# A four-layer cross-attention kernel on one core: another order around the third layer's MLP

## The chip, the cores and the metric

One core of a Trainium2 chip runs the whole kernel. The metric is the device time of one launch in microseconds. Everything is float32 at the interface; TensorE (PE) multiplies, VectorE (DVE), ScalarE (ACT) and GpSimd (POOL) do the rest, and SyncE (SP) issues the transfers.

## What is computed

Eight sequences `b` of 256 tokens, width 256, pass through four cross-attention layers that all look at the same context of 8 x 64 tokens. The third layer (called layer 2 here, counted from 0) is the one that matters:

```python
x = layer_norm(hidden_states, ln1_w, ln1_b)
q, k, v = x @ q_w + q_b, ctx @ k_w + k_b, ctx @ v_w + v_b      # 16 heads of 16
attn = softmax(where(mask, q @ k.T * scale, lowest))
hidden = (attn @ v) @ cproj_w + cproj_b + hidden_states
y = layer_norm(hidden, ln2_w, ln2_b)
y = gelu(y @ fc_w + fc_b, approximate=True) @ proj_w + proj_b  # the MLP, 256 -> 1024 -> 256
x = hidden + y
```

Layer 0 and layer 1 are attention alone; the fourth layer has two cross-attentions with 16 heads of 128 and an MLP of its own.

## The kernel before, in words

**Slots.** Layers 0 to 2 are cut into 24 units, one for each layer and sequence, so units 16 to 23 are layer 2. Every engine runs the same loop over slots `u = 0..25`, each with its own list of steps written out by hand, and semaphores alone tie the engines together. An engine works its list strictly in order. A unit of layer 2 has two tiles of 128 x 1024 scores. In slot `u` TensorE does: scores of unit `u`, `source(u+2)` (transposes of the normalised input into `work[2]`, L436), `values(u+1)` (L481), `probs_transposed` (L561), `reciprocals_transposed(u-1)` into `work[3]` (L575), `weighted(u-1)` (L594), `queries(u+1)` (L518) and last `output(u-1)` (L610). VectorE does in slot `u`: `mlp_weight_low(u-18)` (L1161), `unit_residual(u-2)` (L1118), in slots 21 to 23 `mlp_stats` (L1004, L1008), `tile_sums` of the last tile (L1092), `unit_reciprocals` (L1099), `tile_max` and `tile_shifted` for two tiles (L1070, L1086) with `mlp_norm` (L1014) between them in slots 21 to 23, `unit_normal(u-1)` (L1105) and `tile_sums` of the first tile. `source(u+2)` in layer 2 waits for `unit_residual(u-2)`, which frees `work[2]`, and for the normalised input of `ln_finish` on ScalarE (L1568). GpSimd halves and quarters the exponentials for the sums (L1898, L1901), spreads the reciprocals (L1888), finishes the variances (`rstd`, L1857 and L1860) and adds bias rows (L1910).

**The MLP in parts.** A float32 product is made of three in a rounded format: high x high, low x high and high x low (L631 to L633). ScalarE rounds (`mlp_weight_high` L1611, `mlp_source_high` L1623, `mlp_hidden` L1722 with the gelu and L1728 with the rounding) and VectorE subtracts to get the low part (`mlp_weight_low`, `mlp_source_low` L1175, `mlp_hidden_low` L1180). The weights are eight pieces; ScalarE rounds piece `u-17` at the end of slot `u`, and VectorE's low part of it stands at the start of slot `u+1`.

**Order around the MLP.** For a sequence `b` there are four `hidden(b, f)` (12 matmuls of 256 columns each, into `fbank[f]`, the two halves of the two score tensors) and one `projected(b)` (48 matmuls, into `work[b % 2]`). In slot 24, with no scores left, TensorE does `mlp_source(0)` (into `fbank[3]`), the last probabilities, `reciprocals_transposed(23)`, `weighted(23)`, `hidden(0,0)` and `output(23)`, then `hidden(0,1..3)` with `mlp_source(1)` before the last. From then on a pass is `hidden(b,0)`, `hidden(b,1)`, `mlp_source(b+1)`, `projected(b-1)`, `hidden(b,2)`, `hidden(b,3)`. `mlp_hidden(0,·)` on ScalarE waits until `output(23)` is done, since its buffers lie over attention buffers.

VectorE's pass `b` is: `mlp_hidden_low(b,0)`, `mlp_affine(b+1)` (L1020), `mlp_hidden_low(b,1)`, `mlp_source_low(b+1)`, then work for the fourth layer's weights, which it does in passes 2 to 6: `wq_biased` in 3 to 6 (L1293, 128 x 1024), `wq_sums` in 2 to 5 (L1285, four) and `value_sums` in 2 to 5 (L1307, four, each on the result of the one before). Then `mlp_residual(b-1)` (L1270), `mlp_hidden_low(b,2)` and `(b,3)`, and `mlp_stats(b+3)` with `mlp_norm(b+3)`, between which VectorE waits for GpSimd's `rstd`. GpSimd has `mlp_bias` (L1910) behind each norm and `wq_scaled` (L1986) behind each `wq_sums`.

**After it.** The fourth layer's loop over `STEPS` starts with `key_projection(0)`, which waits until all MLP residuals are done (`d_mr`), and `key_projection(1)` (L775), then `key_products(0)`, `key_products(1)` (L847). On ScalarE `key_bias(1)` (L1758) stands behind the copies of `key_products(0)` (L1768). SyncE loads the fourth layer's value weights when `projected(7)` is done, since they lie over the MLP's weights.

## Time and profile before

| what | value |
| --- | --- |
| median of 3 runs | 1130.79 us (1129.34 to 1131.52) |
| the profiled execution: its own time / its span | 1130.49 / 1128.4 us |
| PE busy | 1033.0 us, 92% |
| DVE busy | 663.2 us, 59% |
| ACT busy | 519.1 us, 46% |
| POOL busy | 402.6 us, 36% |

The rows further down are of this profiled execution, times in us from the start of its span; 2.1 us of its time lie outside the span. The share of the whole hides the stage: slots 18 to 24 of the loop run from about 303 to 391 us, the MLP from there to about 501 us. In a timeline row the bracket holds how long the engine was idle before the operation and what released it. PEclk is the granted TensorE clock as a share of 2.4 GHz.

### The profile page before, as it was taken

Reading aid. Unit: us, or ns where it says so; the run is one execution under the profiler, and the core shown is the slowest. Engines: PE = TensorE matmul, PEld = TensorE weight load, DVE = VectorE, ACT = ScalarE, POOL = GpSimd, SP = SyncE. Lnnn points to the kernel's source line nnn. Section 1 sums busy time; section 2 is a strip of 40 time slices with the busy share of each in tenths; the row PEclk is TensorE's granted clock in tenths of the full one; section 3 lists DMA queues with packets and bytes.
Section 4 is the critical chain, followed back from the end, with each engine's and each line's share of the span. In section 5 each row is a group of like instructions: output and inputs, shape, how many; then the busy total and the mean of one; then the engine's idle time right before and its main releaser. Section 6 shows DMA issues by size and latency. Waiting matters only on the chain.

```text
span 1128.4 us, 17672 instructions
## 1 busy us (share of the span) xinstructions
PE 1033.0 (92%) x7036; PEld 810.7 (72%) x7036; DVE 663.2 (59%) x1127; ACT 519.1 (46%) x1036; POOL 402.6 (36%) x416
## 2 busy tenths in 40 slices
PE   6999889887789799989999999999999999978997
PEld 3666555555566699887787777777777777648997
DVE  3657888778568669722444545775444454574552
ACT  2556777676566454433333332333323333324543
POOL 2534578688966523200222112331122211222230
PEclk9999999998999999999999999999999999999999
DMA  9000000000000060010000013310000000100000
GB/s 307 36 2 1 1 1 1 1 1 1 1 1 1 24 220 1 1 53 23 1 1 1 1 49 102 112 38 1 1 1 1 1 1 7 69 1 1 29 19 29
DMA packets 17046, 32.26 MB, mean 29 GB/s; under 512 B 3522, under 2 KB 8388, under 8 KB 16452
## 3 DMA queue, kind: packets, MB, share of 16 engines
q1 hardware_dynamic: 16964, 31.13, 8.1%
q8 instruction: 56, 0.92, 0.3%
q14 instruction: 26, 0.21, 0.1%
HBM read 29.03 MB, written 2.10 MB: 28 GB/s over the span
## 4 chain that ended last, share of the span: by engine, by line
PE 74%; ACT 8%; POOL 7%; issue 5%; DVE 5%; DMA 0%; POOLq 0%; DVEq 0%; ACTq 0%
PE work L775 10%; PE work L891 10%; PE scores L830 9%; PE work L847 5%; PE work L880 4%; PE work L561 3%; PE work L631 3%; PE work L632 3%; PE work L633 3%; PE scores L631 3%; PE scores L633 3%; PE scores L632 2%; PE work L518 2%; PE work L862 2%; PE work L436 2%
## 5 line engine op out<-in xcount | busy, mean ns | idle before, releaser
L891 PE MATMUL work<-pair,probsT 128*128 128x256 f32 x512 | 120.3, 388 | 11.0 <-ACT pair L1777 8.8
L1857 POOL TENSOR_SCALAR stat<-stat 128x2 f32<-128x2 f32 (+1 forms) x49 | 11.1, 227 | 315.4 <-DVE stat L1008 313.9
L891 PEld LDWEIGHTS work<-pair,probsT 128*128 128x128 f32 x512 | 95.7, 192 | 35.3 <-issue 20.3
L775 PE MATMUL work<-ctxT,w 128*128 128x128 f32 x1008 | 118.2, 275 | 2.7 <-ACT pair L1777 1.1
L775 PEld LDWEIGHTS work<-ctxT,w 128*128 128x128 f32 x1008 | 116.3, 192 | 4.1 <-issue 2.0
L830 PE MATMUL scores<-pair,act_bufs 128*128 128x512 f32 x256 | 115.2, 592 | 0.0
L1768 ACT ACTIVATE pair<-work 128x512 f32<-128x512 f32 x64 | 38.2, 598 | 154.5 <-PE work L847 154.5
L1758 ACT ACTIVATE kvT<-work,cols 128x128 f32<-128x128 f32 x124 | 35.5, 369 | 153.2 <-PE work L775 153.2
L2005 POOL TENSOR_TENSOR probs<-probs,smax 128x1024 f32<-128x1024 f32 x22 | 42.0, 1907 | 157.6 <-DVE smax L1398 157.6
L1378 DVE TENSOR_REDUCE smax<-scores 128x16 f32<-128x1024 f32 x32 | 39.2, 1225 | 77.2 <-PE scores L830 77.2
L830 PEld LDWEIGHTS scores<-pair,act_bufs 128*128 128x128 f32 x256 | 46.3, 190 | 46.0 <-issue 45.9
L1369 DVE TENSOR_TENSOR kvT<-work,cols 128x512 f32<-128x512 f32 x32 | 22.1, 691 | 93.1 <-PE work L775 93.1
L847 PEld LDWEIGHTS work<-kvT,w 128*128 128x128 f32 x512 | 61.9, 192 | 15.4 <-issue 15.4
L1070 DVE TENSOR_REDUCE smax<-scores 128x16 f32<-128x1024 f32 x48 | 57.9, 1205 | 20.1 <-PE scores L552 19.4
L847 PE MATMUL work<-kvT,w 128*128 128x128 f32 x512 | 62.4, 275 | 1.8 <-ACT kvT L1758 1.8
L880 PE MATMUL work<-w,kvT 128*64 128x256 f32 x512 | 62.3, 385 | 0.0
L561 PEld LDWEIGHTS work<-ident,pair 128*128 128x128 f32 x256 | 30.0, 150 | 40.6 <-ACT pair L1579 30.6
L561 PE MATMUL work<-ident,pair 128*128 128x128 f32 x256 | 37.7, 294 | 22.1 <-ACT w L1586 13.3
L1586 ACT ACTIVATE w<-work 128x512 f32<-128x512 f32 x88 | 47.6, 593 | 14.4 <-PE work L561 14.3
L1910 POOL TENSOR_TENSOR x<-x,rows_late 128x512 f32<-128x512 f32 x32 | 50.2, 1572 | 9.9 <-DVE act_bufs L1014 8.2
L1014 DVE TENSOR_SCALAR act_bufs<-x,stat 128x256 f32<-128x256 f32 x58 | 44.0, 800 | 14.9 <-POOL stat L1860 14.9
L1898 POOL TENSOR_TENSOR pair<-probs 128x512 f32<-128x512 f32 x32 | 40.9, 1278 | 29.8 <-ACT probs L1579 29.6
(194 smaller groups left out, 2634.0 us busy)
## 6 DMA issues: line engine op xcount, KB each, us to landing
w<-in_l_wk SPq DMA_DIRECT2D x8, 512.0 KB, 6.1
w<-in_l_wq SPq DMA_DIRECT2D x8, 512.0 KB, 6.7
w<-in_l_wo SPq DMA_DIRECT2D x8, 512.0 KB, 7.5
w<-in_l_wv SPq DMA_DIRECT2D x8, 512.0 KB, 5.4
out<-x SPq DMA_DIRECT2D x8, 256.0 KB, 2.2
x<-in_x SPq DMA_DIRECT2D x1, 1536.0 KB, 9.3
pair<-in_l_fc SPq DMA_DIRECT2D x1, 1024.0 KB, 7.1
pair<-in_l_pr SPq DMA_DIRECT2D x1, 1024.0 KB, 9.1
```

Source lines behind the costliest of these rows:

```text
L561: last = tr(work[half][:, q * P:(q + 1) * P], probs[k % 4][:, (4 * half + q) * P:(4 * half + q + 1) * P], ident[:, :])
L631: mm(bank, s_hi, m_hi, start=start, stop=False)
L632: mm(bank, s_hi, m_lo, start=False, stop=False)
L633: return mm(bank, s_lo, m_hi, start=False, stop=stop)
L775: last = mm(bank[:, h * P:(h + 1) * P], w[:, c, (4 * g + h) * K3:(4 * g + h + 1) * K3], ctxT[:, c, p * P:(p + 1) * P], start=(c == 0), sto ...
L830: last = mm(sc[j % 2][:, half * BANK:(half + 1) * BANK], fixed[j // 2 % 2][:, c, t * P:(t + 1) * P], pk[n % 2][:, bb, c, half * BANK:(half ...
L847: last = mm(step_banks(j)[2 + c][:, h * P:(h + 1) * P], w3_wq[:, 4 * g + h, c * P:(c + 1) * P], kvT[i % 2][:, h, :], start=True, stop=True)
L880: last = mm(bank[h * S:(h + 1) * S, bb * D:(bb + 1) * D], kvT[2][:, 2 * q + h, bb * S:(bb + 1) * S], w3_wo[:, 4 * g + 2 * q + h, :], start ...
L891: last = mm(step_banks(j + 1)[0][:, 0:D], probsT_bufs[j % 2][:, q, :], pv[n % 2][:, bb, q, :], start=(q == 0), stop=(q == GH // 2 - 1))
L1070: v.tensor_reduce(smax[k % 2][:, 0:GH], s3, X, ALU.max).then_inc(d_max, 1)
L1586: act(pT[:, 4 * half:4 * half + 4, t, :], work[half][:, :].rearrange("p (q n) -> p q n", n=P), ACT.Copy).then_inc(a_pT, 1)
L1910: g.tensor_tensor(xb(b), xb(b), row(name).unsqueeze(1).broadcast_to([P, TT, D]), ALU.add).then_inc(done, 1)
```

## The change

1. Slots 18 to 25: `mlp_weight_low` moves from the start of VectorE's slot to its end.
2. `mlp_source(0)` moves from slot 24 to slot 23, ahead of `output(22)`, and from `fbank[3]` to `work[3]`; `reciprocals_transposed(23)` now waits for its affine step. VectorE's `mlp_affine(0)` stands first in slot 24 and `mlp_source_low(0)` ahead of the last tile's sums; ScalarE's `mlp_source_high(0)` ahead of the last `probs_out`.
3. `hidden(0,0)` goes ahead of `reciprocals_transposed(23)`, `hidden(0,1)` in between `weighted(23)` and `output(23)`; both wait for the second last tile alone.
4. Statistics and norm of sequence 2 leave slot 23: a pass `b` of the MLP now does `mlp_stats(b+2)`, `mlp_norm(b+2)`, and in another place.
5. A pass on TensorE is `hidden(b,0)`, `hidden(b,1)`, `mlp_source(b+1)`, `hidden(b,2)`, `projected(b-1)`, `hidden(b,3)`. VectorE takes `mlp_hidden_low(b,2)` ahead of statistics, norm and the weight work, and `mlp_residual(b-1)`, `mlp_hidden_low(b,3)` last. GpSimd takes `wq_scaled` behind `mlp_bias`.
6. `key_projection(0)` and `(1)` go ahead of `projected(7)`, into `fbank[0]` and `fbank[1]`, and wait for the gelus of those banks; the wait for all residuals moves to the steps behind.

```diff
         def key_bank(i):
-            return fbank[0] if i == 1 else step_banks(i - 4)[0]
+            return fbank[i] if i < 2 else step_banks(i - 4)[0]
...
+        def mlp_bank(b):
+            return work[3] if b == 0 else work[2 + b % 2]
...
+                if u == NU - 1:
+                    e.wait_ge(d_mT, 2)
...
-                    e.wait_ge(d_seen, NK)
+                    e.wait_ge(a_rT, NU - 1)
...
-                    e.wait_ge(d_seen, NK)
+                    e.wait_ge(d_seen, NK - 1 + f // 2)
...
-                    if u == NU:
-                        mlp_source(0)
                     for k in late:
                         probs_transposed(k)
                     if tiles:
                         scores(*tiles_of(u)[1])
+                    if u == NU:
+                        hidden(0, 0)
                     if u > 0:
                         reciprocals_transposed(u - 1)
                         weighted(u - 1)
                     if u == NU:
-                        hidden(0, 0)
+                        hidden(0, 1)
...
+                if u == NU - 1:
+                    mlp_source(0)
                 if u > 0:
                     output(u - 1)
...
-            for f in range(1, 4):
-                hidden(0, f)
-                if f == 2:
-                    mlp_source(1)
-            for b in range(1, B + 1):
-                for f in range(2):
-                    if b < B:
-                        hidden(b, f)
+            hidden(0, 2)
+            mlp_source(1)
+            hidden(0, 3)
+            for b in range(1, B):
+                hidden(b, 0)
+                hidden(b, 1)
                 if b + 1 < B:
                     mlp_source(b + 1)
+                hidden(b, 2)
                 projected(b - 1)
-                for f in range(2, 4):
-                    if b < B:
-                        hidden(b, f)
+                hidden(b, 3)
...
-                if i == 0:
-                    e.wait_ge(d_mr, B)
-                if i == 1:
-                    e.wait_ge(a_g, 4 * B)
+                if i < 2:
+                    e.wait_ge(a_g, 4 * (B - 1) + i + 1)
...
+            for i in range(2):
+                key_projection(i - 4, i)
+            projected(B - 1)
...
-                for q in mlp_pieces(u - 1):
-                    mlp_weight_low(q)
+                if u == NU:
+                    mlp_affine(0)
                 if u >= 2:
                     unit_residual(u - 2)
-                if NU - 3 <= u < NU:
+                if u == NU:
+                    mlp_source_low(0)
+                if NU - 3 <= u < NU - 1:
                     mlp_stats(u - NU + 3)
-                if u == NU:
-                    mlp_affine(0)
...
-                if NU - 3 <= u < NU:
+                if NU - 3 <= u < NU - 1:
                     mlp_norm(u - NU + 3)
...
-                if u == NU:
-                    mlp_source_low(0)
                 if tiles:
                     tile_sums(tiles[0][0])
+
+                for q in mlp_pieces(u - 1):
+                    mlp_weight_low(q)
...
-            for b in range(B + 1):
-                if b < B:
-                    mlp_hidden_low(b, 0)
+            for b in range(B):
+                mlp_hidden_low(b, 0)
                 if b + 1 < B:
                     mlp_affine(b + 1)
-                if b < B:
-                    mlp_hidden_low(b, 1)
+                mlp_hidden_low(b, 1)
                 if b + 1 < B:
                     mlp_source_low(b + 1)
+                mlp_hidden_low(b, 2)
+                if b + 2 < B:
+                    mlp_stats(b + 2)
+                    mlp_norm(b + 2)
...
                 if b > 0:
                     mlp_residual(b - 1)
-                for f in range(2, 4):
-                    if b < B:
-                        mlp_hidden_low(b, f)
-                if b + 3 < B:
-                    mlp_stats(b + 3)
-                    mlp_norm(b + 3)
+                mlp_hidden_low(b, 3)
+            mlp_residual(B - 1)
...
+                    if u == NU:
+                        mlp_source_high(0)
                     for k in late:
                         probs_out(k)
...
-            for b in range(3):
+            for b in range(2):
                 mlp_bias(b)
-            for b in range(3, B):
-                if b >= 5:
-                    wq_scaled(1, b - 5)
+            for b in range(2, B):
                 rstd(("m2", b), TT)
                 mlp_bias(b)
-            wq_scaled(1, 3)
+                if b >= 4:
+                    wq_scaled(1, b - 4)
```

## Rows read from the trace of the kernel before

**Rows 1.** What TensorE waited for, 290 to 520 us: total, times, longest.

```profile
PE work L436 <- DVE x L1118: 7.8, 4, 3.5
PE work L631 <- ACT m_hid_high L1728: 6.5, 3, 2.4
```

**Rows 2.** Timeline, slot 18: start, duration, engine, operation, [idle before, releaser].

```profile
305.12 1.09 ACT L1568 ACTIVATE act_bufs<-x,stat 128x256 f32<-128x256 f32 x2 [2.38 <-POOL stat L1866]
...
306.76 0.89 DVE L1161 TENSOR_TENSOR m_w_low<-pair,m_w_high 128x512 fp32r<-128x512 f32 x1 [5.17 <-ACT m_w_high L1611]
...
308.31 0.66 PE L436 MATMUL work<-ident,act_bufs 128*128 128x128 f32 x4 [3.53 <-DVE x L1118]
...
308.89 1.98 PE L481 MATMUL work<-w,ctxT 128*64 128x256 f32 x8
```

**Rows 3.** Timeline, slot 20, 334 to 335 us.

```profile
334.25 0.68 DVE L1118 TENSOR_TENSOR x<-work,x 128x512 f32<-128x512 f32 x1
...
334.98 0.66 PE L436 MATMUL work<-ident,act_bufs 128*128 128x128 f32 x4 [1.42 <-DVE x L1118]
```

**Rows 4.** Timeline, slots 23 and 24, 373 to 387 us.

```profile
373.43 1.13 DVE L1014 TENSOR_SCALAR act_bufs<-x,stat 128x256 f32<-128x256 f32 x2
...
377.60 3.42 PE L610 MATMUL work<-w,pair 128*128 128x256 f32 x8 [1.85 <-DVE pair L1105]
...
379.53 1.06 POOL L1901 TENSOR_TENSOR pair<-pair 128x256 f32<-128x256 f32 x1
...
381.06 0.69 DVE L1118 TENSOR_TENSOR x<-work,x 128x512 f32<-128x512 f32 x1 [1.05 <-PE work L610]
...
384.09 0.66 PE L575 MATMUL work<-ident,pair 128*128 128x128 f32 x4 [1.76 <-POOL pair L1888]
...
386.42 0.68 DVE L1175 TENSOR_TENSOR m_src_low<-act_bufs,m_src_high 128x512 fp32r<-128x512 f32 x1
```

**Rows 5.** Timeline behind `output(23)`, 390 to 398 us.

```profile
390.70 1.28 ACT L1722 ACT_TABLE_LOAD   x1 [4.80 <-PE work L610]
...
392.86 0.63 ACT L1728 ACTIVATE m_hid_high<-pair 128x512 fp32r<-128x512 f32 x1
...
393.40 0.82 ACT L1722 ACTIVATE pair<-scores,cols 128x256 f32<-128x256 f32 x2
...
397.62 0.55 PE L631 MATMUL scores<-m_src_high,m_w_high 128*128 128x256 f32 x1 [2.29 <-ACT m_src_high L1623]
```

**Rows 6.** Windows: stretch, length, busy us of PE, PEld, DVE, ACT, POOL, then PEclk.

```profile
397.62:401.00 3.38, 3.38 (x16) 3.38 (x17) 2.12 (x7) 1.01 (x3) 0.95 (x2) 0.50 1.01 384
402.06:414.00 11.94, 11.94 (x103) 11.94 (x102) 6.90 (x12) 6.12 (x14) 1.00 (x1) 1.00 0.82 321
439.44:453.64 14.20, 12.81 (x95) 12.84 (x96) 12.95 (x28) 4.85 (x11) 5.17 (x4) 0.88 0.01 2
```

**Rows 7.** Timeline of VectorE and GpSimd in the MLP's `b = 4`.

```profile
442.75 0.74 DVE L1014 TENSOR_SCALAR pair<-x,stat 128x256 f32<-128x256 f32 x2 [1.14 <-POOL stat L1860]
...
446.30 1.22 DVE L1293 TENSOR_TENSOR w<-w,pair 128x1024 f32<-128x1024 f32 x1
...
449.06 4.06 DVE L1307 SCALAR_TENSOR_TENSOR pair<-w,cols,pair 128x256 f32<-128x256 f32 x4
...
443.56 1.66 POOL L1910 TENSOR_TENSOR x<-x,rows_late 128x512 f32<-128x512 f32 x1 [0.85 <-DVE pair L1014]
449.23 2.58 POOL L1986 TENSOR_TENSOR w<-w,pair 128x1024 f32<-128x1024 f32 x1 [4.00 <-DVE pair L1285]
```

**Rows 8.** One line's view: `value_sums` at L1307, duration min/median/max in ns.

```profile
L1307 DVE SCALAR_TENSOR_TENSOR pair<-w,cols,pair x30: 466/485/2506, 421.2 to 771.4; 128x256 f32<-128x256 f32 x30
```

**Rows 9.** Timeline at the end of the MLP, 501 to 511 us.

```profile
501.68 2.02 PE L775 MATMUL work<-ctxT,w 128*128 128x128 f32 x16 [0.87 <-DVE x L1270]
...
509.08 2.02 PE L847 MATMUL work<-kvT,w 128*128 128x128 f32 x16 [1.81 <-ACT kvT L1758]
```

**Rows 10.** DMA issues on the page: KB each, median us to landing.

```profile
w<-in_l_wv SPq DMA_DIRECT2D x8, 512.0 KB, 5.4
```

More of the change, by code:

```diff
@@ L645, in mlp_source @@
                     e.wait_ge(d_mT, 2 * (b - 2) + 2)
-                transposes(fbank[3] if b == 0 else work[2 + b % 2], norm[(B + b) % 3]).then_inc(pe_mx, 1)
+                transposes(mlp_bank(b), norm[(B + b) % 3]).then_inc(pe_mx, 1)
             def hidden(b, f):
@@ L779, in first_free @@
             def first_free(j):
+                e.wait_ge(d_mr, B)
                 e.wait_ge(a_pk, 2 * keys_before(j))
@@ L785, in second_free @@
             def second_free(j):
+                e.wait_ge(d_mr, B)
                 e.wait_ge(a_pk, 2 * keys_before(j))
@@ L790, in third_free @@
             def third_free(j):
+                if j > -4:
+                    e.wait_ge(d_mr, B)
                 e.wait_ge(a_lk, keys_before(j))
@@ L794, in fourth_free @@
             def fourth_free(j):
+                if j > -4:
+                    e.wait_ge(d_mr, B)
                 e.wait_ge(d_vT, values_before(j))
@@ L907, in value_constants @@
                 mm(step_banks(j)[1][:, 0:D], ones[:, :], value_sum, start=True, stop=True).then_inc(pe_bias, 1)
+            for i in range(2):
+                key_projection(i - 4, i)
+            projected(B - 1)
             for j in STEPS:
                 key, value, i = key_of(j), value_of(j), input_of(j)
-                if key is not None and key != 1:
+                if key is not None and key >= 2:
                     key_projection(j, key)
-                if key == 0:
-                    key_projection(j + 1, 1)
                 if value is not None:
@@ L1169, in mlp_affine @@
                     e.wait_ge(a_sh, b - 2)
-                affine(fbank[3] if b == 0 else work[2 + b % 2], srcT[i % 3], "l2_g2", "l2_b2", d_mT)
+                affine(mlp_bank(b), srcT[i % 3], "l2_g2", "l2_b2", d_mT)
             def mlp_source_low(b):
@@ L1688, in scalar @@
                         exponentials(tiles[0])
-                if u == NU:
-                    mlp_source_high(0)
                 if u > 0:
@@ L1730, in scalar @@
             for b in range(B):
-                mlp_hidden(b, 0)
-                mlp_hidden(b, 1)
-                if 0 < b and b + 1 < B:
-                    mlp_source_high(b + 1)
-                mlp_hidden(b, 2)
-                if b == 0:
-                    mlp_source_high(1)
+                for f in range(3):
+                    mlp_hidden(b, f)
+                    if f == (2 if b == 0 else 1) and b + 1 < B:
+                        mlp_source_high(b + 1)
                 mlp_hidden(b, 3)
@@ L1970, in gpsimd @@
                     reciprocals_spread(u - 1)
-                if NU - 3 <= u < NU:
+                if NU - 3 <= u < NU - 1:
                     rstd(("m2", u - NU + 3), TT)
```

## The prediction

> **What bounds the kernel now.** I read the waits of TensorE first, since the table has it busy for 92% of the span: from 290 to 520 us two entries stand out, `source` waiting for `unit_residual` (L436, 7.8 us in four waits) and `projected` waiting for the low hidden parts (L631, 6.5 us in three) [rows 1]. Then the timeline at each of them. In slot 18 the transposes start at 308.31 after 3.53 us of idle TensorE. The engine named is VectorE, but its residual is itself queued behind `mlp_weight_low` (L1161), which had stood idle 5.17 us for ScalarE's rounded piece [rows 2]. In slot 20 the same order costs 1.42 us [rows 3], and so it does in 19 and 21 (7.8 - 3.53 = 4.27 = 3 x 1.42) [rows 1, 3]. In slots 23 and 24 VectorE's own list is the chain. In the MLP one pass takes 14.20 us, of which VectorE is busy 12.95 and waits 1.14 for GpSimd's `rstd`; that is the whole of it, while TensorE needs 11.94 us for a pass [rows 6, 7]. So passes 3 to 5 go by VectorE, although the waits name ScalarE.
>
> **Part 1, low weight parts at the slots' ends.** Slot 18: the residual can start when `output(16)` is done, about 303.7. Next late is the normalised input of `source(20)`, which ScalarE finishes at 305.12 + 1.09 = 306.2 [rows 2]. The transposes go at 306.3 instead of 308.31: 2.0 us. Behind the long wait TensorE ran at half clock: `values` took 1.98 us [rows 2], eight matmuls that run in about 1.1 at full clock; the matmuls behind them in the same 3.4 us lose another 0.5. With a wait of 1.5 us left, like the 1.42 in slot 20, I take this away too: 1.4 us, bounds 0 and 1.4, the upper because the row it is nearest to, slot 20, shows no such loss. Slots 19 to 21: the residual starts with the end of `output`, 1.2 us ahead of the end of the scores that TensorE does meanwhile, so the transposes follow without a gap: 4.3 us. TensorE is then the bound there, at 12.55 - 1.42 = 11.1 us a slot; VectorE has 8.6 to 9.7 of work. The moved subtraction itself (0.89 in [rows 2]) falls into VectorE's idle time at the slot's end; its input is by then a slot old. In slots 21 and 22 VectorE leads or starts 0.3 us sooner: 0.5 together. Sum of part 1: 2.0 + 1.4 + 4.3 + 0.5 = 8.2.
>
> **Part 2, slots 23 and 24.** VectorE's list in slot 23 loses `mlp_stats(2)` (0.9) and `mlp_norm(2)` (1.1, L1014) [rows 4]. `output(22)` waits for `unit_normal(22)` at the end of this list (1.85 us, behind another short wait, and then 3.42 us at half clock for eight matmuls that take 1.9) [rows 4]. It starts 1.85 us sooner, at 375.75 on the old time scale, now with `mlp_source(0)` in the gap before it, and ends at 377.7, not 381.0. From there on VectorE: sums, the low part, `mlp_affine(0)` (1.0) to 377.7, `unit_residual(22)` to 378.4, `mlp_source_low(0)` (0.68) [rows 4] to 379.1, sums of the last tile (GpSimd done by 378.7; before, 379.53 + 1.06 = 380.6 [rows 4]), reciprocal at 379.8, GpSimd's spread 380.45. TensorE: last probabilities, `hidden(0,0)` from 379.15 to 380.6, `reciprocals_transposed(23)` at 380.6 (was 384.09 [rows 4]), weighted to 382.25, `hidden(0,1)` to 383.7, `output(23)` to 385.6. Before, `hidden(0,0)` stood behind `mlp_source_low(0)` at 386.42 [rows 4] and `output(23)` ended at 390.6. Gain 5.0. `hidden(0,1)` delays `output(23)` by 0.7, which is in the sum. The new wait of `reciprocals_transposed(23)` for the affine step has `weighted`, `hidden(0,1)` and `output(23)` behind it; the step is done 2.8 us earlier, so it costs nothing, and at most the step's 1.0 if that lead were gone. On ScalarE the last `probs_out` stands behind `mlp_source_high(0)`, which waits for that same step until 377.7; the transposes that it copies come at 378, so nothing is lost.
>
> **Part 3, up to `hidden(1,0)`.** Nothing is gained. `hidden(1,0)` needs source 1, and ScalarE starts on that only after a table load of 1.28, three gelus (0.82) with three roundings (0.63), all behind `output(23)` [rows 5]: 397.62 - 390.6 = 7.0 us, before and after. TensorE only waits longer for it, 3.6 us for 2.29, and then runs at half clock as now (16 matmuls in 3.38 us, PEclk 0.50 [rows 6], a loss of 1.5).
>
> **Part 4, the MLP's passes.** Three `hidden` ahead of `projected` give TensorE 1.43 us more cover. But the bound is VectorE's pass, and its list doesn't get shorter. It is 14.20 [rows 6], plus two things. First, `mlp_hidden_low(b,2)` now stands directly behind `mlp_source_low`, where before the weight work stood: ScalarE needs 0.63 for the source, 0.82 and 0.63 for the gelu [rows 5], VectorE has 1.3 us of work meanwhile, so it waits 0.8. Second, GpSimd's `mlp_bias` (L1910) starts just behind the norm [rows 7]; before, short steps lay beside it, now `wq_biased` and `wq_sums` do. What such a meeting costs VectorE the trace shows for `value_sums`: 0.485 us each, but up to 2.506 [rows 8], and four take 4.06 while GpSimd's 2.58 us run begins [rows 7], so VectorE stands still for GpSimd's whole instruction. For `wq_sums` (L1285) there is no such meeting in the trace. Bounds: 0, or the 1.25 us that L1910 runs; a little below 0 (-0.2) if the short steps now go free of it. I take 1.25, since L1307 reads two float32 operands from SBUF just as L1285 does. Pass: 14.20 + 0.8 + 1.25 = 16.25. Statistics now lie in passes 2 to 5 beside the weight work, so three such periods follow on pass 2. Counted from `hidden(1,0)`: VectorE starts pass 2 at 16.5 and needs 14.5 (as above without `wq_biased`) up to `mlp_hidden_low(2,3)`; `projected(2)`, which TensorE reaches at 30.1, starts at 31.8, `projected(5)` at 31.8 + 3 x 16.25 = 80.5. Behind it TensorE is the bound: 5.84 + 1.5 (half clock after a wait of 4) + 4 x 1.43 + 5.84 + 1.43 + 3.7 (two key projections) + 5.84 = 29.9, to 110.4. Before, the same work ended at 501.68 + 2 x 1.9 [rows 9] = 505.5, or 107.9. So the passes lose 2.5, after they got back 5 us at the end, where the wait ahead of `projected(7)`, its half clock and the 0.87 us for the residual [rows 9] go.
>
> The Trainium skill has a rule for this meeting (page SBUF — State Buffer, section "Who interferes with whom"): a VectorE instruction with two inputs in SBUF contends with a GpSimd instruction that reads SBUF, and the one that issued first blocks the other for its whole length. L1307 agrees. By the rule `wq_sums` would be blocked as well, the 16.25; without it the pass would be 15.0.
>
> **Part 5, the key projections.** `key_products(0)` can follow `projected(7)` at once, but `key_bias(1)` stands behind its copies on ScalarE's list as before, so the 1.81 us wait of L847 [rows 9] stays. The residual of sequence 7 (0.7) hides behind `key_products(0)` (1.8). The value weights' transfers are issued with the end of `projected(7)`, as before; they land 5.4 us after issue [rows 10], and `value_projection(0)` now comes 8.2 us behind it instead of 12.9: nothing, or up to 1 us if the first lands late. All behind that shifts as a whole.
>
> **Sum.** 8.2 + 5.0 + 0 - 2.5 + 0 = 10.7 us. The profiled execution took 1130.49 (span 1128.4, the rest outside), 0.3 below the median. 1130.5 - 10.7 = 1119.8 us.
>
> **Rivals.**
> A. `wq_sums` isn't held up by GpSimd. For it: none of its instructions shows it; against: L1307 [rows 8]. Four passes are 1.25 shorter: 1114.8.
> B. The slots don't close. What is late next there (ScalarE's `ln_finish`, the exponentials, GpSimd, idle only 0.5 us between some steps in slot 18) takes the place of the residual, and slot 18 keeps its half clock: 4.3 + 1.4 less, 1125.5.
> C. The cover does all that it could and TensorE sets the passes: `projected(5)` at 30.1 + 3 x 11.94 = 65.9, the end at 94.3: 13.6 gained where I lose 2.5, 1103.7. Against it stands VectorE's 12.95 us of work in a pass [rows 6], over 11.94.
> D. Slower. TensorE now stands 4.3 us ahead of each `projected` in four passes and 3.6 ahead of `hidden(1,0)`. If the clock stays at the lower of its two levels (1.2 GHz) for the whole pass, a pass takes 2 x 11.94 = 23.9, over 16.25: 7.6 each, 30 us in four, 1150. It makes the kernel slower from 15 us at the lower level in each pass on (half of it lost, less the 4.3 idle, four times, over 10.7 + 2.3). Against it: after waits of 2.3 to 3.5 us the clock was back within 3.4 us [rows 2, 6].
> E. Gains and losses cancel (B with a longer list on VectorE than counted): 1130.
>
> **How the numbers follow.** About 0.2% can be told from no change here. Forecast 0.50 (own range 1117 to 1122.5), A 0.22 (1112 to 1117), B 0.15 (1123 to 1127.5), C 0.03, D 0.05, E 0.05. Leaving out C, D, E and the outer part of B gives 1112.5 to 1126. Faster by over 0.2%: 0.50 + 0.22 + 0.15 + 0.03 = 0.90; same 0.05; slower 0.05.
>
> **What would show it.** Right: no wait of L436 on L1118 above 0.3 us in slots 19 to 21, 306.3 for the transposes in slot 18, `output(23)` ending 13 us sooner, `projected(2)` to `projected(5)` 16.2 us apart with waits of 3 to 4 us ahead of them, L1285 with durations above 1.5 us, no wait ahead of `projected(7)`, the 1.8 us wait of L847 still there. Wrong: passes of 15.0 (A), of 12 (C), or long matmuls through a whole pass (D).

## The result and the profile after

The changed kernel takes **1119.29 us** (median of 4 runs, 1118.81 to 1119.43) where the kernel before took 1131.15 beside it (4 runs, 1129.34 to 1131.60): ratio 0.9897, 95% interval 0.9880 to 0.9914. It is 1.0% faster, 0.5 us from the forecast of 1119.8. Its profiled execution took 1119.15 us, with a span of 1117.0 (before: 1130.49 and 1128.4).

The span falls into four parts, cut at three starts that every kernel here has: `output(16)`, `output(23)` and the first key product. The last columns are the lengths between the cuts. All experiments are in it too, since most verdicts below are read here. Each row is one profiled execution; in e2 and e9 it is the fastest of four, 4.2 and 3.1 us or more under the other three.

| kernel | output(16) starts | to output(23) | to the first key product | to the end | span |
|---|---|---|---|---|---|
| before | 301.70 | 87.00 | 116.62 | 623.08 | 1128.4 |
| **changed** | 303.31 | 74.03 | 116.67 | 622.99 | 1117.0 |
| e1_low_first | 303.93 | 81.79 | 119.23 | 626.05 | 1131.0 |
| e2_low_last_alone | 302.15 | 77.61 | 112.25 | 623.19 | 1115.2 |
| e3_narrow_bias | 301.96 | 74.01 | 115.34 | 623.39 | 1114.7 |
| e4_old_passes | 302.84 | 75.23 | 112.55 | 625.78 | 1116.4 |
| e5_keys_behind | 302.86 | 74.02 | 121.81 | 627.81 | 1126.5 |
| e6_spread | 302.64 | 74.02 | 103.63 | 625.11 | 1105.4 |
| e7_spread_early | 302.32 | 74.02 | 102.13 | 623.23 | 1101.7 |
| e8_old_slot24 | 302.57 | 75.18 | 115.70 | 625.85 | 1119.3 |
| e11_delay_1 | 302.12 | 74.02 | 120.23 | 625.13 | 1121.5 |
| e9_delay_2 | 302.72 | 74.06 | 118.43 | 624.69 | 1119.9 |
| e10_delay_4 | 302.14 | 74.05 | 120.04 | 625.87 | 1122.1 |

Of the 11.4 us, 12.97 were gained in slots 18 to 24 (87.00 to 74.03), nothing in the MLP (116.62 and 116.67), and nothing in the fourth layer (623.08 and 622.99). The first column lost 1.6: the changed execution was already 1.37 us later at its first `output` (41.83 for 40.46). The three delay kernels, whose code is the changed kernel's up to there, have that row at 40.77 to 41.25, so the first stage differs by about a microsecond between executions of the same order of work.

The waits of TensorE from 290 to 515 us, changed kernel (total, times, longest), answer to [rows 1]:

```profile
PE work L637 <- issue: 10.0, 4, 3.9
PE work L440 <- ACT act_bufs L1576: 4.1, 2, 2.5
PE scores L637 <- ACT m_src_high L1631: 3.7, 1, 3.7
PE work L856 <- issue: 1.8, 1, 1.8
```

The residual is gone from the list: `source` (now L440) waits for the normalised input alone. The waits ahead of `projected` (L637 to `work`) grew to 10.0 us and are put down to "issue". What ends them is VectorE's low hidden part: in the pass shown below the two at 433.09 take 1.28 us together, the first is done at about 433.8, and `projected(3)` starts at 433.87.

Slot 18, timeline (start, duration, engine, operation, idle before and releaser), answers to [rows 2]:

```profile
305.24 0.69 DVE L1128 TENSOR_TENSOR x<-work,x 128x512 f32<-128x512 f32 x1 [2.04 <-PE work L616]
...
306.71 1.09 ACT L1576 ACTIVATE act_bufs<-x,stat 128x256 f32<-128x256 f32 x2 [2.37 <-POOL stat L1871]
...
307.95 0.63 PE L440 MATMUL work<-ident,act_bufs 128*128 128x128 f32 x4 [1.57 <-ACT act_bufs L1576]
...
308.51 1.08 PE L485 MATMUL work<-w,ctxT 128*64 128x256 f32 x8
```

The residual starts as soon as `output` ends, the wait fell from 3.53 to 1.57, and `values` runs in 1.08 us at full clock (1.98 before). Behind `output(23)`, answering to [rows 5] and [rows 6] (in the second fence: stretch, length, busy us of PE, PEld, DVE, ACT, POOL, then PEclk, the granted clock):

```profile
379.34 1.28 ACT L1730 ACT_TABLE_LOAD   x1 [3.30 <-PE work L616]
...
386.26 0.51 PE L637 MATMUL scores<-m_src_high,m_w_high 128*128 128x256 f32 x1 [3.72 <-ACT m_src_high L1631]
```

```profile
433.87:449.90 16.03, 13.65 (x101) 13.48 (x101) 13.98 (x28) 6.26 (x13) 5.72 (x4) 0.89 0.01 2
```

A pass takes 16.03 us now. VectorE is busy 13.98 of it, and most of the rest are two waits (0.70 and 1.14 us) that its timeline shows. The rows are from the pass ahead of that window, `b = 3`, VectorE and then GpSimd, answering to [rows 7]:

```profile
421.37 0.69 DVE L1190 TENSOR_TENSOR m_hid_low<-pair,m_hid_high 128x512 fp32r<-128x512 f32 x1 [0.70 <-ACT m_hid_high L1736]
...
424.09 0.74 DVE L1024 TENSOR_SCALAR act_bufs<-x,stat 128x256 f32<-128x256 f32 x2 [1.14 <-POOL stat L1865]
424.74 1.22 DVE L1303 TENSOR_TENSOR w<-w,pair 128x1024 f32<-128x1024 f32 x1
425.87 1.53 DVE L1295 CUSTOM_DVE_ANT_0 pair<-w,pair,cols 128x256 f32<-128x256 f32 x1
...
427.33 0.47 DVE L1295 CUSTOM_DVE_ANT_0 pair<-w,pair,cols 128x256 f32<-128x256 f32 x1
...
428.55 4.02 DVE L1317 SCALAR_TENSOR_TENSOR pair<-w,cols,pair 128x256 f32<-128x256 f32 x4
...
433.09 1.28 DVE L1190 TENSOR_TENSOR m_hid_low<-pair,m_hid_high 128x512 fp32r<-128x512 f32 x2
...
424.91 2.21 POOL L1915 TENSOR_TENSOR x<-x,rows_late 128x512 f32<-128x512 f32 x1 [0.85 <-DVE act_bufs L1024]
428.71 2.54 POOL L1991 TENSOR_TENSOR w<-w,pair 128x1024 f32<-128x1024 f32 x1 [1.59 <-DVE pair L1295]
```

And the end of the MLP, TensorE, answering to [rows 9]: no wait for the residual is left, that of the key products is.

```profile
494.01 1.95 PE L856 MATMUL work<-kvT,w 128*128 128x128 f32 x16
497.72 2.02 PE L856 MATMUL work<-kvT,w 128*128 128x128 f32 x16 [1.76 <-issue]
```

### The profile page after: what moved, and what is told of

Same layout as the page of the kernel before. It is cut to its first block, busy times and chain, and to the rows that moved or that the text cites. A ratio compares the mean times of both kernels' runs of the same rounds, so it can differ in the third digit from the quotient of the medians.

```text
span 1117.0 us, 17673 instructions
## 1 busy us (share of the span) xinstructions
PE 1030.6 (92%) x7036; PEld 809.2 (72%) x7036; DVE 663.2 (59%) x1127; ACT 518.3 (46%) x1036; POOL 403.5 (36%) x416
## 4 chain that ended last, share of the span: by engine, by line
PE 76%; ACT 7%; POOL 7%; issue 5%; DVE 4%; DMA 0%; POOLq 0%; DVEq 0%; ACTq 0%
PE work L900 10%; PE work L780 10%; PE scores L839 10%; PE work L856 5%; PE work L889 4%; PE work L565 3%; PE work L637 3%; PE work L638 3%; PE work L639 3%; PE scores L637 3%; PE work L522 3%; PE scores L639 3%; PE scores L638 3%; PE work L616 2%; PE work L440 2%
## 5 line engine op out<-in xcount | busy, mean ns | idle before, releaser
L565 PE MATMUL work<-ident,pair 128*128 128x128 f32 x256 | 36.5, 288 | 20.1 <-ACT w L1594 11.9
L1594 ACT ACTIVATE w<-work 128x512 f32<-128x512 f32 x88 | 47.4, 592 | 10.7 <-PE work L565 10.7
```

The costliest lines, as they stand in the source:

```text
L565: last = tr(work[half][:, q * P:(q + 1) * P], probs[k % 4][:, (4 * half + q) * P:(4 * half + q + 1) * P], ident[:, :])
L1594: act(pT[:, 4 * half:4 * half + 4, t, :], work[half][:, :].rearrange("p (q n) -> p q n", n=P), ACT.Copy).then_inc(a_pT, 1)
```

## Experiments: what each part is worth

The expectations number the parts as the six items of the section on the change; the prediction's part 4 is items 4 and 5, its part 5 is item 6.

**Item 1 taken back.** The low weight parts stand ahead of the residual again, all else as changed.

```
                     tile_shifted(*tiles[0])
+                for q in mlp_pieces(u - 1):
+                    mlp_weight_low(q)
                 if u == NU:
                     mlp_affine(0)
...
-                for q in mlp_pieces(u - 1):
-                    mlp_weight_low(q)
```

> The changed kernel (1119.3 us) with the low weight parts back at the start of VectorE's slots 18 to 25, all else as changed. My account: what queues the residual behind ScalarE's rounded piece is this position alone, worth 2.0 + 1.4 in slot 18, 1.42 each in slots 19 to 21 and 0.5 in 21 and 22, so 8.2 us are lost: 1127.5 us, and source(20) to source(23) again wait on the residual (about 3.5, 1.4, 1.4, 1.4). Rival: most of the slots' gain comes from elsewhere or is given back at the MLP's passes, which VectorE sets: 1120 to 1122 us.

Measured: 1133.02 us (6 runs, 1130.14 to 1136.21), ratio to before 1.0018 (0.9998 to 1.0037). The whole gain is gone, which is more than item 1. The table says which share is its own: the slots take 81.79 for 74.03, 7.8 us (expected 8.2), and the waits for the residual are back:

```profile
PE work L440 <- DVE x L1128: 7.2, 4, 3.0
```

The other 5.6 us (2.56 up to the first key product, 3.06 behind it) lie where no order was changed. `projected(5)` to `projected(6)` took 13.06 us for 11.56 and `output(23)` to `projected(0)` 16.31 for 15.24, for the same matmuls: TensorE's clock, taken up below.

**Item 1 alone**, in the kernel before: the same two lines moved to the slot's end, nothing else.

> The kernel before (1131.2 us) with this one edit alone, the low weight parts at the end of the slots. My account: 8.2 us, 1123.0 us, output(20) about 8 us earlier, and the rest of the kernel shifted as a whole with MLP passes of 14.2 us as before. Rival: the gain needs the new order of slots 23 and 24 behind it, 1127 us or more.

Measured: 1121.52 us (4 runs, 1117.27 to 1121.66), ratio 0.9907 (0.9889 to 0.9926). The slots went from 87.00 to 77.61: item 1 alone is worth 9.4 us of the 12.97, and 7.8 when it comes last, since in slots 23 and 24 it and item 4 relieve the same list. The passes stayed at 14.2 us. The MLP was 4.4 shorter than in the kernel before though its order is the same; three stretches of half clock of some 1.45 us each did not come in this execution. It took 1117.27 us at a mean granted clock of 0.986, the other three executions of the same kernel 1121.48 to 1121.66 at 0.982. By the medians item 1 alone gives 10.0 us (1131.49 beside it) and all six items 11.9.

**Items 2 and 3 taken back**: source 0 and the first two slices of the hidden layer at their old places, on all engines.

```
+                    if u == NU:
+                        mlp_source(0)
                     for k in late:
                         probs_transposed(k)
...
-                    if u == NU:
-                        hidden(0, 0)
                     if u > 0:
                         reciprocals_transposed(u - 1)
                         weighted(u - 1)
                     if u == NU:
-                        hidden(0, 1)
+                        hidden(0, 0)
...
-                if u == NU - 1:
-                    mlp_source(0)
                 if u > 0:
                     output(u - 1)
```

> The changed kernel with source 0 and the first two hidden quarters back at their places of before (transposes in slot 24 into fbank[3], hidden(0,0) behind weighted(23), hidden(0,1) behind output(23), and VectorE's and ScalarE's steps with them). My account: what slot 23 gains stays (statistics and norm of sequence 2 are still gone from it), but the last tile's sums again stand behind the affine step and hidden(0,0) again waits for the low source part ahead of output(23): output(23) 1.7 to 3 us later, hidden(1,0) the same 7.0 us behind its end, 1121.5 us, give or take 3 for the clock. Rival: the quarters themselves (2 x 1.43 us of work moved ahead) are the gain, then hidden(1,0) comes 3 us later and projected(0) as well: 1124 us.

Measured: 1121.43 us (4 runs, 1120.88 to 1121.54), ratio 0.9913 (0.9892 to 0.9935). `output(23)` comes 1.15 us later (75.18 for 74.03; 1.7 to 3 were expected), and TensorE waits once more for GpSimd's spread:

```profile
373.14 0.66 PE L579 MATMUL work<-ident,pair 128*128 128x128 f32 x4 [1.77 <-POOL pair L1890]
...
386.67 0.36 PE L635 MATMUL scores<-m_src_high,m_w_high 128*128 128x256 f32 x1 [2.29 <-ACT m_src_high L1628]
```

But up to the first key product the two kernels differ by 0.2 us (190.88 and 190.70 from `output(16)`). The longer wait ahead of `hidden(1,0)`, 3.72 for 2.29, isn't what takes the gain away: ScalarE's chain is as long as ever, and `hidden(1,0)` starts 8.9 us behind the start of `output(23)` in both. What takes it is the clock behind the wait. From `hidden(1,0)` to `projected(0)`, changed kernel, then this one:

```profile
386.26:392.58 6.32, 6.32 (x41) 6.32 (x41) 4.60 (x11) 3.50 (x7) 2.62 (x3) 0.73 1.02 404
386.67:392.00 5.33, 5.04 (x40) 4.83 (x41) 4.10 (x11) 3.44 (x7) 2.86 (x3) 1.00 1.02 383
```

The kernel before has the wait of 2.29 too, with half clock behind it, so which wait loses its clock isn't settled by its length. The medians differ by 2.1 all the same; in the spans 2.9 us of difference lie in the last stage, whose order is the same. That 1121.43 meets the expected 1121.5 is luck.

**Items 4 and 5 taken back**: three quarters ahead of the projection given up, statistics three sequences ahead again, `wq_scaled` at its old place (VectorE's part of the edit):

```
                 if b + 1 < B:
                     mlp_source_low(b + 1)
-                mlp_hidden_low(b, 2)
-                if b + 2 < B:
-                    mlp_stats(b + 2)
-                    mlp_norm(b + 2)
...
                 if b > 0:
                     mlp_residual(b - 1)
+                mlp_hidden_low(b, 2)
+                if b + 3 < B:
+                    mlp_stats(b + 3)
+                    mlp_norm(b + 3)
                 mlp_hidden_low(b, 3)
```

> The changed kernel with the passes of the MLP as before on all engines (projected ahead of hidden 2 and 3, VectorE's low parts 2 and 3, statistics and norm last, statistics of sequence 2 back in slot 23, GpSimd's order too); key projections ahead of projected(7) and slot 24 stay as changed. My account: VectorE sets the passes, 14.2 us each instead of 16.0, so this edit by itself costs and undoing it gains: output(23) 2.0 later, from hidden(1,0) to the key products 103.2 instead of 107.8, so 2.5 us faster than the changed kernel, 1116.8 us. Rival: three quarters ahead of a projection give TensorE 1.4 us of cover in each of three waits, so undoing it costs 2 to 4 us: 1121 to 1123 us.

Measured: 1118.45 us (4 runs, 1113.72 to 1119.09), ratio 0.9880 (0.9859 to 0.9901), no difference from the changed kernel that the medians can show. The stages can: the passes are 14.2 us again, `output(23)` is 1.2 later, and the stretch up to the first key product is 112.55 for 116.67, 4.1 us shorter. The last stage took 2.8 more. Where the change gave the projection more cover, it made the kernel 2.9 us slower from `output(16)` to the key products (187.78 and 190.70; 2.5 were expected); the last stage hides it. The clock hides another 1.5: `projected(5)` to `projected(6)` took 13.05 us in e4 and 11.56 in the changed kernel, for the same amount of work.

**Item 6 taken back**: both key projections behind the last projection, as they were.

> The changed kernel with the first two key projections back behind projected(7) and their waits as before. My account: projected(7) then waits 2.3 us for the last low part, runs its first 3.4 us at half clock (1.5 us) and the key projection waits 0.9 for the residual: 4.7 us slower, 1124.0 us. Rival: the wait only moves, to ScalarE's key bias or the value weights' transfers: 1120 us.

Measured: 1128.33 us (8 runs, 1126.23 to 1130.16), ratio 0.9971 (0.9959 to 0.9983). Up to the first key product it takes 5.1 us more (121.81 for 116.67), as its timeline explains: the wait, the half clock behind it (`projected(7)` takes 7.5 us, 6.0 in the changed kernel), and the residual come back (4.7 expected for the three).

```profile
486.71 0.35 PE L637 MATMUL work<-m_w_high,m_hid_high 128*128 128x256 f32 x1 [2.36 <-ACT m_hid_high L1738]
495.05 2.02 PE L780 MATMUL work<-ctxT,w 128*128 128x128 f32 x16 [0.88 <-DVE x L1282]
```

The last stage is 4.8 longer again, which the 4.7 didn't have: 1128.33 for the expected 1124.0.

## Experiments: what sets a pass

**Is `wq_sums` held up by GpSimd?** The bias instruction of sequences 4 to 7 is cut to 8 of 256 columns in both tiles (128x16), so that it is over before `wq_sums` begins.

```
-                add_row(b, "l2_pb", p_xm)
+                if b >= 4:
+                    g.tensor_tensor(xb(b)[:, :, 0:8], xb(b)[:, :, 0:8],
+                                    row("l2_pb")[:, 0:8].unsqueeze(1).broadcast_to([P, TT, 8]), ALU.add).then_inc(p_xm, 1)
+                else:
+                    add_row(b, "l2_pb", p_xm)
```

> The changed kernel, but mlp_bias of sequences 4 to 7 adds only 8 of the 256 columns (the rest of that bias is left out). My account: wq_sums (L1295) is held up by GpSimd's bias addition for its whole length, so its longest duration falls from 1.52 to about 0.5 us, and a pass of VectorE from 16.0 to 15.0 us, in four passes: 4.2 us less up to the first key product, if the clock's part is the same. Rival: the first wq_sums is long for another reason (it follows wq_biased, whose result it may wait for), then it stays at 1.5 and the passes at 16.0.

Measured: 1116.06 us (2 runs, 1115.32 and 1116.79), ratio 0.9867 (0.9838 to 0.9896). The passes are 15.0 us (`projected(2)` to `(5)` at 416.76, 431.76, 446.75, 461.75) for 16.02. The line's view (duration min/median/max in ns), changed kernel first, then this one:

```profile
L1295 DVE CUSTOM_DVE_ANT_0 pair<-w,pair,cols x32: 472/481/1527, 410.0 to 727.9; 128x256 f32<-128x256 f32 x32
```

```profile
L1295 DVE CUSTOM_DVE_ANT_0 pair<-w,pair,cols x32: 475/480/485, 409.9 to 725.2; 128x256 f32<-128x256 f32 x32
```

With the meeting away none of the 32 takes longer than 485 ns; with it one in each of four passes takes 1.51 to 1.53 us. That is the lock (one engine standing still for the other's instruction), 1.05 us a pass, shown by taking its cause away. The Trainium skill's rule (page SBUF — State Buffer, section "Who interferes with whom"), that two inputs in SBUF suffice to be blocked by GpSimd's reading instruction, agrees. Only 1.33 us of the expected 4.2 arrived at the first key product: `projected(5)` to `projected(6)` took 13.04 us for 11.56, and `output(23)` to `projected(0)` 16.50 for 15.24, so that `projected(2)` came no sooner (40.79 us behind `output(23)` for 40.54) and only three of the four shorter passes counted. Both are the clock again.

**VectorE's passes evened out.** If its list is the bound, then 12 us passes need less on it: the statistics ahead of the low source part, so that GpSimd's `rstd` runs beside it, and the `value_sums` of the second half moved to the two last passes, where VectorE has room.

```
                 mlp_hidden_low(b, 1)
+                if b + 2 < B:
+                    mlp_stats(b + 2)
                 if b + 1 < B:
                     mlp_source_low(b + 1)
-                mlp_hidden_low(b, 2)
                 if b + 2 < B:
-                    mlp_stats(b + 2)
                     mlp_norm(b + 2)
+                mlp_hidden_low(b, 2)
...
                     wq_sums(1, b - 2)
-                    value_sums(1, b - 2)
+                if b >= 6:
+                    value_sums(1, 2 * b - 12)
+                    value_sums(1, 2 * b - 11)
```

> The changed kernel with VectorE's passes evened out: statistics ahead of the low source part, the norm behind it, and all value_sums in passes 6 and 7 instead of 2 to 5. My account: VectorE's list sets passes 2 to 5, and it falls from 16.0 to about 12.3 us (the 4.06 for value_sums go, 0.8 and 0.6 of waits are filled, but GpSimd's wq_scaled now holds up the last low part by 1.8), so projected(2) to projected(5) take 37 us instead of 48, with 1.3 less ahead of projected(2): about 12 us faster than the changed kernel, 1107 us, give or take 3 for the clock. Rival: the passes are set by the handover from ScalarE to VectorE or by GpSimd, then they stay above 14 us and the time at 1113 or more.

Measured: 1108.42 us (4 runs, 1107.24 to 1109.13), ratio 0.9799 (0.9780 to 0.9818). The stretch from `output(23)` to the first key product fell by 13.0 us, and TensorE has no idle time left in the passes (window views of this kernel, two passes; columns as above):

```profile
415.61:427.52 11.91, 11.91 (x103) 11.91 (x101) 10.80 (x23) 6.25 (x13) 6.50 (x4) 1.00 0.00 0
427.52:439.53 12.01, 12.01 (x102) 11.90 (x101) 11.09 (x23) 6.27 (x13) 6.50 (x4) 1.00 0.01 1
```

So with the cover of three quarters the passes go by TensorE, as in rival C, once VectorE's list fits into 11.9 us. The lock is still there (the first `wq_sums` takes 1.52 us), and now costs nothing. How much of the gain the shorter list would have brought under the old order of the passes, no run shows.

**The table load ahead of `output(23)`.** On top of that, a one-column gelu behind slot 24's work on ScalarE makes the table load early, and source 1 is rounded after the second gelu, not the third.

```
+                if u == NU:
+                    act(tanh_gate[:, :], tanh_gate[:, :], ACT.Gelu_apprx_tanh)
...
-                    if f == (2 if b == 0 else 1) and b + 1 < B:
+                    if f == 1 and b + 1 < B:
                         mlp_source_high(b + 1)
```

> The kernel e6_spread, and besides a one-column gelu on ScalarE at the end of slot 24, so that the table load falls into its idle time, and mlp_source_high(1) ahead of the third gelu. My account: hidden(1,0) waits for ScalarE's chain behind output(23); it loses the table's 1.28 and one gelu with rounding, 1.4, so the wait falls from 3.7 to about 1.0 us and with it the half clock behind it (1.5): 3 to 4 us faster than e6_spread, 1103.5 us. Rival: VectorE's affine and low parts are late next, then 1 to 2 us.

Measured: 1104.75 us (4 runs, 1103.49 to 1105.69), ratio 0.9767 (0.9747 to 0.9786), **the fastest of all**, 2.3% under the kernel before. Its timeline:

```profile
375.06 1.28 ACT L1721 ACT_TABLE_LOAD   x1
...
383.65 0.36 PE L637 MATMUL scores<-m_src_high,m_w_high 128*128 128x256 f32 x1 [2.13 <-issue]
```

The load is over when `output(23)` starts (376.34), and `hidden(1,0)` waits 2.13 us, not 3.72. This is what part 3 left lying. The stretch to the key product fell by 1.5 (103.63 to 102.13); of the rest of the span's 3.7 us, 1.9 come from the last stage. So the rival came true, 1 to 2 us, and not my account, which had a wait of 1.0 and no half clock behind it (from `hidden(1,0)` to `projected(0)` it takes 6.3 us, 6.2 in e6): VectorE's low source part is late next. It ends at 383.55, 1.4 us behind ScalarE's rounding (382.15), since the statistics of sequence 2 now stand ahead of it.

```profile
381.52 0.63 ACT L1634 ACTIVATE m_src_high<-act_bufs 128x512 fp32r<-128x512 f32 x1 [0.27 <-DVE act_bufs L1030]
...
382.88 0.67 DVE L1185 TENSOR_TENSOR m_src_low<-act_bufs,m_src_high 128x512 fp32r<-128x512 f32 x1
```

## Experiments: a last stage that differs by 3 to 5 us

In the table's last column the same code takes 622.99 to 627.81 us. I compared starts in the fourth layer: from its first tile to tile 29 all kernels agree to 0.03 us. Then the steps come: tile 29 to tile 30 is 12.16 us in most kernels and 13.84 in e5, e6, e9 and e11. Two more come behind the last tile, 1.4 to 1.6 and 1.4 to 1.5 us, both in e1, e4, e5, e8 and e10; the other kernels have 0.4 or less there. The waits of TensorE are the same. What differs is the clock behind them. To test whether the moment decides, I lengthened the changed kernel by a constant: key projection 0 is computed half, once or twice more ahead of the counted one. This is the edit for twice:

```
                     e.wait_ge(a_g, 4 * (B - 1) + i + 1)
...
+                if i == 0:
+                    for _ in range(2):
+                        project(w3_wk, i, key_bank(i))
                 project(w3_wk, i, key_bank(i)).then_inc(pe_kp, 1)
```

> The changed kernel with half of key projection 0 done once more ahead of the counted one (four of its eight matmuls, about 0.9 us of TensorE; the copies, key products and everything else wait for it as before). In the kernels run so far the waits of TensorE behind the first key product were the same, to 0.1 us, and yet that last part took from 623.0 to 627.8 us, because the half clock behind some waits came in some kernels and not in others. Theory 1, when such a wait falls in time decides whether the clock drops: the waits stay as they are and the time is that of the changed kernel plus 0.9 plus 0 to 3 times about 1.45 us, 1120.2 to 1124.6. Theory 2, it belongs to the kernel's order of work: the time is the changed kernel's plus 0.9, 1120.2 within 0.4.

> The same with the whole of key projection 0 once more, about 1.9 us. Theory 1, the moment decides: 1121.2 plus 0 to 3 times 1.45 us, and not the same number of them in this kernel as in the one with 0.9 us and the one with 3.7. Theory 2, the order decides: 1121.2 within 0.4, the last part as long as in the changed kernel.

> The same with key projection 0 twice more, about 3.7 us. Theory 1, the moment decides: 1123.0 plus 0 to 3 times 1.45 us. Theory 2, the order decides: 1123.0 within 0.4. If all three kernels are longer by just their delay, theory 1 has no support, and the 3 to 5 us by which the last part differed between the earlier kernels stay open.

The delays put in were 0.90, 1.79 and 3.57 us by `projected(6)` to `projected(7)`. Measured:

| | median (range), 4 runs | above the changed kernel | less the delay |
|---|---|---|---|
| e11_delay_1 | 1123.18 (1121.57 to 1123.28) | 3.9 | 3.0 |
| e9_delay_2 | 1125.02 (1121.67 to 1125.44) | 5.7 | 3.9 |
| e10_delay_4 | 1124.27 (1122.42 to 1125.46) | 5.0 | 1.4 |

The kernel with the longest delay is no slower than the middle one, though 1.8 us more were put into it, and executions of one and the same kernel lie 3.8 us apart (1121.67 at a mean granted clock of 0.982, 1125.44 at 0.979). The kernel before took 1131.68 beside these three and 1131.15 beside the changed kernel, so about 0.5 of each surplus may not be theirs. None of the medians is longer by its delay within 0.4, so theory 2 falls. Theory 1 fits: the surplus is 1 to 3 steps of about 1.45 us, and not the same number in the three. That the moment decides is argued from this; what it is about the moment, no run shows. The same rows of the changed kernel, then of e11, then of e10 (timeline, TensorE, the last tiles and the last MLP):

```profile
974.53 3.69 PE L900 MATMUL work<-pair,probsT 128*128 128x256 f32 x16 [2.28 <-ACT pair L1782]
...
1001.86 1.97 PE L871 MATMUL work<-ident,probs 128*128 128x128 f32 x8 [6.11 <-POOL probs L2009]
1004.51 5.19 PE L900 MATMUL work<-pair,probsT 128*128 128x256 f32 x16 [0.69 <-ACT probsT L1794]
...
1012.66 0.36 PE L637 MATMUL scores<-src_high,w_high 128*128 128x256 f32 x1 [2.52 <-ACT src_high L1828]
```

```profile
976.89 5.38 PE L902 MATMUL work<-pair,probsT 128*128 128x256 f32 x16 [2.28 <-ACT pair L1784]
...
1005.90 1.97 PE L873 MATMUL work<-ident,probs 128*128 128x128 f32 x8 [6.10 <-POOL probs L2011]
1008.56 5.61 PE L902 MATMUL work<-pair,probsT 128*128 128x256 f32 x16 [0.69 <-ACT probsT L1796]
```

```profile
976.77 3.69 PE L903 MATMUL work<-pair,probsT 128*128 128x256 f32 x16 [2.28 <-ACT pair L1785]
...
1006.77 6.58 PE L903 MATMUL work<-pair,probsT 128*128 128x256 f32 x16 [0.69 <-ACT probsT L1797]
...
1016.30 0.55 PE L637 MATMUL scores<-src_high,w_high 128*128 128x256 f32 x1 [2.52 <-ACT src_high L1831]
```

Behind the same wait of 2.28 us the 16 matmuls take 3.69, 5.38 and 3.69 us. Behind the same 6.1 us they take 5.19, 5.61 and 6.58. Behind the same 2.52 us the 24 matmuls that follow take 3.10 us in the changed kernel (first one 0.36) and 4.47 in e10 (first one 0.55). One such stretch costs 1.4 to 1.7 us, or little (0.4 for the 5.61), or nothing. In the passes it costs nothing even where it comes: the windows of the pass ahead of `projected(5)` and of the work behind it, changed kernel, then e11:

```profile
449.90:465.90 16.00, 13.62 (x100) 13.41 (x100) 13.95 (x28) 6.25 (x13) 5.72 (x4) 0.89 0.01 1
465.95:472.00 6.05, 6.05 (x51) 6.05 (x52) 4.56 (x8) 1.99 (x4) 0.00 (x0) 1.00 0.00 0
```

```profile
449.90:465.90 16.00, 12.14 (x100) 11.98 (x101) 13.95 (x28) 6.25 (x13) 5.67 (x4) 1.00 0.00 1
465.95:472.00 6.05, 6.05 (x38) 6.05 (x39) 4.48 (x7) 1.99 (x4) 0.00 (x0) 0.72 0.00 0
```

`projected(5)` starts at 465.9 in both, since VectorE sets that. Ahead of it e11 lost nothing (clock 1.00, 12.14 us busy for 13.62), waited longer for it (3.84 us for 2.42), and then ran at 0.72, where each microsecond counts. The changed kernel had it the other way round.

## Why the prediction was right, step by step

**Part 1: right in sum and in most terms.** Slot 18, from `output(16)` to `output(17)`, fell from 16.24 to 12.67: 3.57 (predicted 3.4, with the half clock away as taken). The transposes came 4.6 us after `output(16)` started, exactly the predicted 306.3 less 301.7. Slots 19 to 21 take 11.06 for 12.55 each, 4.47 (4.3), with no wait for the residual left. Slot 22: 0.39 (0.5).

**Part 2: right in size, a little high.** `output(22)` came 1.95 us sooner within its slot (1.85), `output(23)` another 2.59 (3.15): 4.5 for 5.0.  Taken back by themselves, items 2 and 3 cost 1.15, and item 4 (statistics and norm in slot 23) 1.2; the rest is shared with item 1 (9.4 alone, 7.8 last). Slots together: 12.97, predicted 13.2.

**Part 3: right.** `output(23)` ends at 379.23, `hidden(1,0)` starts at 386.26: 7.03 (7.0), with the wait at 3.72 (3.6) and half clock behind it.

**Part 4: mechanism right, sum wrong by 2.5.** The pass is 16.02 (16.25): 0.70 of stall at the gelu (0.8) and 1.05 for the lock (1.25). GpSimd's bias had itself begun inside `wq_biased` (L1303, until 425.96) and ran 2.21 us, to 427.12; `wq_sums`, issued at 425.87, ended behind it. `projected(2)` came at 31.6 after `hidden(1,0)` (31.8), `projected(5)` at 79.7 (80.5). The mis-sized term stands behind it: "1.5 (half clock after a wait of 4)". The wait was 2.42, and `projected(5)` took 5.98 us at full clock, whereas `projected(3)` and `(4)` had taken 7.48 and 7.47. The first key product came at 107.75 (110.4) where the kernel before has 107.7, so the part cost 0, not 2.5: 0.8 from shorter passes and 1.5 from a clock that stayed up, with about 0.3 in smaller steps. As e1, e3 and e11 show, with 13.04 to 13.06 us from `projected(5)` to `(6)` for 11.56 and the same order of the passes, this 1.5 was luck and not a property of the change. It can still be the same in all four executions of the changed kernel, since they lie within 0.6 us of each other.

**Part 5: right.** The wait of the key products stayed (1.76 for 1.81), the one ahead of `projected(7)` went. Taking it back cost 5.1 us up to the first key product, for "5 us at the end".

**Sum.** Predicted 10.7, measured 11.4 by the spans, 11.9 by the medians. Two errors of opposite sign stand in it: part 4 was 2.5 better, and the first 300 us of the changed execution were 1.6 longer, which no edit caused. That the sum came within 1.2 us is luck to that extent; the mechanism of each part held. Of the rivals, A (1114.8) fell with `wq_sums` at 1.53 us; e3, which makes A's condition true, gave 1116.06. B fell with the slots at 11.06 us; D fell with a clock of 0.89 over a pass; C came true in e6, by a shorter list on VectorE: its first key product comes 94.7 us after `hidden(1,0)` starts (385.58), where C had 94.3.

What the prediction lacked is a rival of the kind "the same order, another clock": a half clock of 1.4 to 1.7 us, on or off behind several waits, which comes to 3 to 5 us for a whole kernel. The range of 13.5 us held it by other terms.

## What to carry to other kernels

Read the list of the engine that ends last, not the name in the wait: here the waits named ScalarE or nobody, and it was VectorE's order (part 1) and length (e6) that paid. More cover for one engine is worth nothing while another's list is longer than the pass: the three quarters ahead, with the order on VectorE that went with them, cost 2.9 us as changed, and together with a list of 11 us instead of 14.0 they are 10 faster than the old order (187.8 to 177.7 from `output(16)` to the first key product, e4 and e6). Which share of these 10 is the cover's wasn't measured. Judge an edit of a few microseconds by the stage it touches, since stages that it doesn't touch moved by up to 5 us.

## What the runs showed of the hardware

Behind one and the same wait of 2.28, 2.52 or 6.1 us TensorE's clock was at half (1.2 for 2.4 GHz) in some profiled executions and not in others. Where it was, the stretches shown cost 0.4 to 1.7 us more, most of them 1.4 to 1.7. No other order of work is needed for it: the changed kernel and its three delayed copies differ in it, and executions of one kernel differ in time and mean granted clock together (e2: 1117.27 us at 0.986, three others 1121.5 at 0.982). The Trainium skill (page TensorE: Matmul & The Clock Gate, Part 1) says of the slow matmuls at a kernel's start that their number varies from run to run. The runs here show such a variation in the middle of a kernel; none was read for the start.

A VectorE instruction with two float32 inputs in SBUF, issued 0.96 us into a GpSimd instruction that reads SBUF, took 1.53 us for 0.47; without the GpSimd instruction beside it none of 32 took over 0.485. It goes the other way round too. `wq_biased` (L1303), issued 0.17 us ahead of GpSimd's bias, took 1.22 us, as it does at 470.04 with no GpSimd instruction beside it, and the bias took 2.21 us, where an addition of the same size at 344.04 takes 1.27. Even the bias cut to 128x16 in e3 took 1.13 us behind `wq_biased`. Changed kernel, then e3:

```profile
344.04 1.27 POOL L1915 TENSOR_TENSOR x<-x,pair 128x512 f32<-128x512 f32 x1
...
470.04 1.22 DVE L1303 TENSOR_TENSOR w<-w,pair 128x1024 f32<-128x1024 f32 x1
```

```profile
423.80 1.13 POOL L1933 TENSOR_TENSOR x<-x,rows_late 128x16 f32<-128x16 f32 x1 [0.85 <-DVE act_bufs L1024]
```

What stays open: which of the waits lose their clock at which moment. The runs show that it is not the length of the wait alone, and no more.
